# One attention stage on TensorE: three score banks instead of two, the turned maxima and the denominators inside the ring of banks, and the value products of two key tiles back to back

## What is computed

```python
qkv = x @ w_qkv + b_qkv
q, k, v = jnp.split(qkv, 3, axis=-1)          # 16 heads of 32, rope on q and k
attn = jnp.einsum('bhqd,bhkd->bhqk', q, k) * (1.0 / np.sqrt(hd))
attn = jax.nn.softmax(attn, axis=-1)
out = jnp.einsum('bhqk,bhkd->bhqd', attn, v)
```

## Time and profile before

| | |
|---|---|
| median of 3 executions | 3583.11 us (3581.57 to 3583.68) |
| profiled execution, its own time | 3584.84 us |
| profiled execution, span of the core | 3583.0 us |
| mean granted TensorE clock | 0.941 of full speed |
| instructions profiled | 53307 |

### The profile page before, as it was taken

How to read it: one execution, slowest core, us unless ns; L and a number is a source line. 1 busy time by engine, 2 the same in 40 slices (tenths; PEclk the granted TensorE clock), 3 DMA queues, 4 the chain that set the end, 5 groups by cost and what they waited for, 6 DMA issues and landing times. The chain is left out here.

```text
span 3583.0 us, 53307 instructions
## 1 busy us (share of the span) xinstructions
PE 3218.5 (90%) x15180; PEld 2074.7 (58%) x15180; DVE 2025.6 (57%) x3254; ACT 1572.8 (44%) x2848; POOL 1665.3 (46%) x732
## 2 busy tenths in 40 slices
PE   5888789999999999999999994433999998999999
PEld 5666644444444444444444442432888886788887
DVE  2887677878777876878787783533322221322222
ACT  1333217676677766777676773233211111211111
POOL 0222318888788887888788886554100000100000
PEclk9999859999999999999999997766999999999999
DMA  4444449898898988899798987554411211411210
GB/s 168 141 141 142 134 91 194 179 195 189 165 196 183 194 176 171 181 188 199 160 194 178 193 191 166 170 182 161 144 47 47 94 47 49 143 66 47 94 47 24
DMA packets 179320, 508.04 MB, mean 142 GB/s; under 512 B 25914, under 2 KB 43434, under 8 KB 145966
## 3 DMA queue, kind: packets, MB, share of 16 engines
q0 software_dynamic: 36240, 248.53, 34.2%
q1 hardware_dynamic: 132308, 233.59, 21.7%
q10 hardware_dynamic: 10512, 22.81, 1.9%
HBM read 175.18 MB, written 93.62 MB: 75 GB/s over the span
## 5 line engine op out<-in xcount | busy, mean ns | idle before, releaser
L733 DVE TENSOR_REDUCE b_mpart<-b_m 128x1 f32<-128x512 f32 x2136 | 1325.9, 685 | 385.2 <-PE b_m L783 381.3
L672 ACT ACTIVATE b_pt<-b_s 128x512 f32<-128x512 f32 x2048 | 1115.0, 596 | 522.3 <-PE b_s L808 466.4
L711 POOL TENSOR_TENSOR b_acc<-b_acc,b_pt 128x2048 f32<-128x2048 f32 x225 | 1049.2, 4663 | 204.9 <-DMA b_pt<-b_pt 204.2
L808 PE MATMUL b_s<-b_qs,b_ks 98*128 98x512 f32 x2050 | 890.9, 435 | 23.7 <-ACT b_pt L672 23.7
L783 PE MATMUL b_m<-b_ks,b_qs 96*128 96x512 f32 x2136 | 787.2, 415 | 20.5 <-issue 20.2
L808 PEld LDWEIGHTS b_s<-b_qs,b_ks 98*128 98x128 f32 x2050 | 387.3, 189 | 675.3 <-ACT b_pt L672 617.5
L860 PE MATMUL b_o<-b_pt,b_vg 128*32 128x512 f32 x4096 | 549.5, 609 | 0.0
L783 PEld LDWEIGHTS b_m<-b_ks,b_qs 96*128 96x128 f32 x2136 | 417.6, 196 | 96.2 <-DVE b_mpart L733 26.3
L1245 DVE SCALAR_TENSOR_TENSOR d_uf<-d_a,keep_chan,d_sg 128x512 f32<-128x512 f32 x128 | 96.1, 751 | 578.1 <-PE d_a L1273 578.1
L1197 POOL DMA_DIRECT2D d_raw<-in_w_fc x32 | 24.0, 755 | 591.7 <-POOLq L1122 495.7
L1216 ACT ACTIVATE d_sg<-d_g,keep_chan 128x512 f32<-128x512 f32 x128 | 88.1, 689 | 419.7 <-PE d_g L1273 419.7
(11 more groups left out here) (130 smaller groups left out, 3606.6 us busy)
## 6 DMA issues: line engine op xcount, KB each, us to landing
b_pt<-b_pt POOLq DMA_DIRECT2D x225, 1024.0 KB, 8.1
b_ks<-scratch_qk_hi SPq DMA_DIRECT2D x36, 512.0 KB, 5.6
b_qs<-scratch_qk_hi SPq DMA_DIRECT2D x68, 256.0 KB, 5.5
scratch_qk_hi<-a_q_hi SPq DMA_DIRECT2D x64, 256.0 KB, 2.5
scratch_qk_lo<-a_q_lo SPq DMA_DIRECT2D x64, 256.0 KB, 2.8
d_h_hi<-scratch_h_hi SPq DMA_DIRECT2D x16, 1024.0 KB, 7.4
d_h_lo<-scratch_h_lo SPq DMA_DIRECT2D x16, 1024.0 KB, 9.6
d_y<-scratch_y SPq DMA_DIRECT2D x16, 1024.0 KB, 8.0
```

Of the source, the lines that this page charges most:

```text
L672: act.activation(pt[:, kt % RING, h, :], ps_s[:, i % LEAD, :], ACT.Exp, scale=SCALE).then_inc(p_ready, 1)
L711: pool.tensor_tensor(acc[slot][:], acc[slot][:], pt[:, (2 * n + 3) % RING, :, :], ALU.add).then_inc(pool_added, 1)
L733: dve.tensor_reduce(mpart[slot][:, i // 4, i % 4:i % 4 + 1], ps_m[:, i % EARLY, :], AX.X, ALU.max).then_inc(max_done, 1)
L808: pe.matmul(ps_s[:, i % LEAD, :], ks[kslot][0:QR, h, kt * P:(kt + 1) * P], qs[qslot][0:QR, h, :], start=True, stop=True).then_inc(st_done, 1)
```

## The change

Six edits go together.

- `LEAD` goes from 2 to 3: three score banks.
- The bank `ps_d` is gone. The denominators take a place in the round of the three score banks (`SUMS_AT` = 35, between the scores of round 7 and of round 8), and the turned maxima a place in the round of the four maximum banks (`TURN_AT` = 3, behind the third maximum product of the unit two ahead).
- The value products of tiles `kt - 1` and `kt` are issued together at the end of odd rounds; even rounds end without one.
- `ORDER` differs between even and odd rounds: `smsmsmms` and `msmsmsms`.
- ScalarE reads the value products of the unit before (L641) behind the fifth exponential of a unit instead of behind the second, and the denominators ahead of exponential 35 instead of behind exponential 35.
- VectorE splits the turned maximum behind the first three reductions of the unit two ahead, not behind the first eight.

```diff
-LEAD = 2
+LEAD = 3
 EARLY = 4
+TURN_AT = 3
+SUMS_AT = 4 * 8 + LEAD
+
+def score_place(i):
+    return i + (i >= SUMS_AT)
+
+def maximum_bank(n, place):
+    return (65 * (n % 8) + place) % EARLY
...
-        ps_s, ps_m, ps_o, ps_d = m.ps("s", LEAD), m.ps("m", EARLY), m.ps("o", 1), m.ps("d", 1)
+        ps_s, ps_m, ps_o = m.ps("s", LEAD), m.ps("m", EARLY), m.ps("o", 1)
...
-        ORDER, TURN = "smsmmsms", 10
+        ORDER, TURN = ("smsmsmms", "msmsmsms"), 10
...
                     for h in range(GH):
                         i = GH * kt + h
+                        if i == SUMS_AT:
+                            read_denominators(u)
                         act.wait_ge(st_done, STEPS * (u + 1) + i + 1)
-                        if kt == 0 and h == LEAD - 1:
+                        if i == GH:
                             read_products(u)
-                    if kt == D_AT + 1:
-                        read_denominators(u)
...
             def scores(n, kslot, qslot, i):
-                pe.wait_ge(p_ready, STEPS * (n + 1) + i + 1 - LEAD)
+                place = score_place(i)
+                if place == SUMS_AT + LEAD:
+                    pe.wait_ge(d_read, n + 2)
+                else:
+                    last = {0: -2, 1: -1, 2: -3}[i] if i < LEAD else i - LEAD + (SUMS_AT < place < SUMS_AT + LEAD)
+                    pe.wait_ge(p_ready, STEPS * (n + 1) + last + 1)
...
                             at += 1
-                    if kt == TURN:
-                        pe.wait_ge(d_read, u + 2)
-                        turn_max(u + 1)
-                    if kt == 0:
+                            if kt == TURN and at == TURN_AT:
+                                turn_max(u + 1, nj)
+                    if kt % 2 == 0:
+                        continue
+                    if kt == 1:
                         pe.wait_ge(o_read, u + 1)
...
-                    pe.wait_ge(p_ready, STEPS * (u + 1) + GH * (kt + 1))
-                    for h in range(GH):
-                        last = pe.matmul(ps_o[h * HD:(h + 1) * HD, 0, :], vg[kslot][:, kt, h * HD:(h + 1) * HD],
-                                         pt[:, kt % RING, h, :], start=kt == 0, stop=kt == NK - 1)
-                    last.then_inc(pv_done, 1)
+                    for n in (kt - 1, kt):
+                        pe.wait_ge(p_ready, STEPS * (u + 1) + GH * (n + 1))
+                        for h in range(GH):
+                            last = pe.matmul(ps_o[h * HD:(h + 1) * HD, 0, :], vg[kslot][:, n, h * HD:(h + 1) * HD],
+                                             pt[:, n % RING, h, :], start=n == 0, stop=n == NK - 1)
+                        last.then_inc(pv_done, 1)
```

More of the change, by code:

```diff
@@ L508, in stage_b @@
         ITEMS = GH * SUB * 4
-        ORDER, TURN = "smsmmsms", 10
+        ORDER, TURN = ("smsmsmms", "msmsmsms"), 10
         PER = ITEMS // NK
         AHEAD = PER * (NK - TURN)
-        assert ORDER.count("m") == PER and ORDER.count("s") == GH
+        assert all(o.count("m") == PER and o.count("s") == GH for o in ORDER)
         D_AT = 7
+        assert SUMS_AT == GH * (D_AT + 1) + LEAD
         def added(u, n):
@@ L645, in read_denominators @@
                 act.wait_ge(d_out, 16 * (u + 1))
-                act.activation(d_sb[:], ps_d[:, 0, :], ACT.Copy).then_inc(d_read, 1)
+                act.activation(d_sb[:], ps_s[:, SUMS_AT % LEAD, :], ACT.Copy).then_inc(d_read, 1)
             def slot_free(u, kt, pair, j):
@@ L750, in _ @@
             finish_max(0, 0)
-            maxima(1, 1, 0, PER)
-            split_max(0)
-            maxima(1, 1, PER, AHEAD)
+            maxima(1, 1, 0, TURN_AT)
+            split_max(0, 0)
+            maxima(1, 1, TURN_AT, AHEAD)
             def body(u, pair, j):
-                at = AHEAD
-                for kt in range(NK):
-                    if kt == TURN:
-                        finish_max(u + 1, (j + 1) % 2)
-                        at = 0
-                    ahead = 1 if kt < TURN else 2
-                    maxima(u + ahead, (j + ahead) % 2, at, at + PER)
-                    at += PER
-                    if kt == TURN + 1:
-                        split_max(u + 1)
-                    if kt == NK - 2:
-                        invert(u)
+                maxima(u + 1, j + 1, AHEAD, ITEMS)
+                finish_max(u + 1, (j + 1) % 2)
+                maxima(u + 2, j + 2, 0, TURN_AT)
+                split_max(u + 1, j + 1)
+                maxima(u + 2, j + 2, TURN_AT, AHEAD - PER)
+                invert(u)
+                maxima(u + 2, j + 2, AHEAD - PER, AHEAD)
             run(dve, body)
@@ L776, in _, with maxima @@
             pe.sem_inc(st_done, STEPS)
-            def maxima(n, kslot, qslot, lo, hi):
+            def maxima(n, j, kslot, qslot, lo, hi):
                 for i in range(lo, hi):
                     h, s, k = i // 16, i // 4 % 4, i % 4
-                    pe.wait_ge(max_done, ITEMS * (n + 1) + i + 1 - EARLY)
-                    pe.matmul(ps_m[:, i % EARLY, :], qs[qslot][0:KR, h, s * P:(s + 1) * P],
+                    place = i + (i >= TURN_AT)
+                    if place == TURN_AT + EARLY:
+                        pe.wait_ge(mlo_ready, n + 1)
+                    else:
+                        last = i - EARLY + (TURN_AT < place < TURN_AT + EARLY)
+                        pe.wait_ge(max_done, ITEMS * (n + 1) + last + 1)
+                    pe.matmul(ps_m[:, maximum_bank(j, place), :], qs[qslot][0:KR, h, s * P:(s + 1) * P],
                               ks[kslot][0:KR, h, k * TB:(k + 1) * TB], start=True, stop=True).then_inc(max_ps, 1)
@@ L788, in denominators @@
                 pe.wait_ge(pool_added, added(u - 1, PAIRS - 1))
-                pe.wait_ge(mlo_ready, u + 2)
-                pe.wait_ge(d_read, u + 1)
                 for h in range(GH):
-                    last = pe.matmul(ps_d[h * HD:(h + 1) * HD, 0, :], ones[:, 0:HD], acc[slot][:, h, :], start=True, stop=True)
+                    last = pe.matmul(ps_s[h * HD:(h + 1) * HD, SUMS_AT % LEAD, :], ones[:, 0:HD], acc[slot][:, h, :], start=True, stop=True)
                 last.then_inc(d_ps, 1)
@@ L814, in _ @@
             operands(0, 0)
-            maxima(0, 0, 0, 0, ITEMS)
+            maxima(0, 0, 0, 0, 0, ITEMS)
             operands(1, 0)
-            maxima(1, 0, 1, 0, PER)
-            turn_max(0)
-            maxima(1, 0, 1, PER, AHEAD)
+            maxima(1, 1, 0, 1, 0, TURN_AT)
+            turn_max(0, 0)
+            maxima(1, 1, 0, 1, TURN_AT, AHEAD)
             pe.wait_ge(ones_ready, 3)
@@ L835, in body @@
                         at = 0
-                    for what in ORDER:
+                    for what in ORDER[kt % 2]:
                         if what == "s":
```

27 lines of the change are left out of this document (15 added, 12 removed).

## The result

Seven executions of the changed kernel had a median of 3566.20 us (3560.90 to 3573.88), seven of the kernel before on the same chip 3583.11 (3579.60 to 3584.86): a ratio of 0.9959, interval 0.9946 to 0.9972. The gain is 17 us, 0.4%, where I had forecast 35 (3548 us). It lies in the range (3504 to 3582), but at rival (b), not at the forecast. The profiled execution took 3560.9 us, 23.9 less than the profiled one of before, with a span of 3559.1. It is the fastest of its seven, as the profiled one of before is nearly the slowest of its own, so the profiles differ by more than the medians. One of the six executions of the queries later took 14096.67 us, and without it that median would be 3559.62 us.

A forecast was written before the change was run, and what follows sets the result against it. TensorE sets the pace, GpSimd with its DMAs close behind. TensorE's unit falls 1.95 us to 48.8, waits eat 0.9, leaving 1.05; over 32 units about 35 us gained, giving 3548 us (range 3504 to 3582).

The forecast's parts named there:

- rival (b): GpSimd and DMA already at their limit over four units; gain 0 to 0.8 us a unit, 3558 to 3583; chance 0.21.
- The pair of rounds: TensorE: pairing value products makes two rounds take 5.86 us instead of 6.20, saving 0.34 a pair, 2.7 a unit.
- 0.15, 0.45 and 0.43: TensorE's unit: microseconds for scores delayed by the denominators' read, the moved read of value products, and the maxima's turn.
- alone it gains nothing: Third score bank: lets ScalarE work through the pair, but no gain by itself since TensorE already starts without a hole.
- The place and the kind of the wait: Exponentials wait for GpSimd's add or a fold, 25 to 35 us in all; maximum products don't wait each pair.
- I give the four units 1.0, 1.9, 0.7 and 0: 0.9 on the mean: TensorE's loss to GpSimd's lateness over four units, three with key/value loads; leaves 1.05 of 1.95 us gained a unit.
- one stretch of GpSimd's chain: Sixth fold's release to the unit's last add: GpSimd and DMA need 25.5 us, TensorE's way shrinks from 26.0 to 24.3.
- ScalarE comes 1.2 us late, and of that TensorE feels about 1.0: At the slot freed by a unit's last add: ScalarE's wait for GpSimd passed on to TensorE, whose bank had 0.45 spare.
- Rival (a): TensorE alone decides, the ring of eight tiles evening out the rest; 1.95 to 2.7 us a unit, 3497 to 3521; chance 0.22.
- Rival (c): Slower: fold landings grow; about 12.3 us in three heavy units uses up the gain, 13.1 gives 3602; chance 0.07.

The follow-up runs named there:

- queries later: Changed kernel with two key/value pieces loaded per unit, queries' load moved behind tile 1's value products and pieces behind tiles 5 and 7: 3559.98 us, ratio 0.9938.
- unpaired kernel: Changed kernel with value products back behind every round, old order and early read of value products; third bank and new places stay: 3577.92 us, ratio 0.9988.
- unpaired kernels: Changed kernel with value products back behind every round, with key/value loads whole (3577.92 us) or cut to four columns (3554.54 us).
- no pieces: Changed kernel with in-loop loads of the next group's keys and values cut to four columns, so later outputs are wrong: 3501.59 us, ratio 0.9778.
- last add first: Changed kernel with GpSimd adding a unit's last pair before issuing the next unit's first fold: 3656.52 us, ratio 1.0202.
- even pieces: Changed kernel with eight key/value pieces spread two to a unit instead of three, three, two and none, first sooner, second later: 3542.15 us, ratio 0.9881.
- half adds: Changed kernel with GpSimd adding only two of four heads, the other denominators left at ones, loads and folds whole: 3509.45 us, ratio 0.9797.

## Why the prediction was right in sign and short in size

**The pair of rounds: right, in part by luck.** 5.82 us for 5.86, 1.85 for both groups and the way back for 1.88. The unhindered unit took 48.30 for 48.8: the pairs give 8 x 0.04 = 0.3 more than forecast, and what I had put at 0.15, 0.45 and 0.43 is 0.86 together, for 1.03. In TensorE's timeline of such units the denominators cost nothing beyond their 0.88, the read of the value products 0.33, and the pair of rounds with the turn takes 6.32, 0.50 more than a plain one (in the unpaired kernel the moved turn costs 0.12, as before). But "alone it gains nothing", of the third bank, was wrong: with the new places it brought a round from 3.10 to 3.05. The unpaired kernels part the gain in another way than I did. From 50.67 to 50.04 us, 0.63 a unit, TensorE's own work fell by bank and places, which my sum had at a loss of 0.48 (0.15 and the turn's 0.33); from 50.04 to 48.22, 1.8 a unit, by the pairs and the read moved with them, which my sum had at 2.44 (2.72 less 0.28). Two errors stood against each other.

**The place and the kind of the wait: right.** ScalarE stands before the slot that the unit's last add frees, for GpSimd, and no maximum product waits in each pair.

**The failed step: "I give the four units 1.0, 1.9, 0.7 and 0: 0.9 on the mean".** It says that of a gain of 1.95 us a unit 0.9 is eaten; inside the passes 2.5 us a unit were eaten out of 2.5 gained, and ScalarE's waits came to 65 us where I said 25 to 35. The path and the wait were the right ones; the term for what they cost was too small. Two things were wrong in it.

First, I followed one stretch of GpSimd's chain, from the sixth fold to the last add, and compared that with TensorE's. The whole unit has to be compared as well. Two folds are under way at most, since fold n + 2 stands behind add n in GpSimd's program. A unit's chain is then: from the first fold to the second over the last add of the unit before, 0.6 + 4.6; three times a landing, 0.2 and an add of 4.57 (second, fourth and sixth fold; the others lie beside them); and the first pair, 4.6. That is 24.1 us and three landings, an estimate from these rows. They took 8.57 us on the mean of these folds in the changed kernel: 49.8 us. With no pieces they sum to 22.7 instead of 25.7: 46.8, under TensorE's 48.3, and the waits inside the passes went. With the last add first they sum to 29.7: 53.8, and the units took 53.96. Units with three pieces had 27.4 to 28.3 in the three landings, about 52; those with two had 24.7, those without 22.4. So three units of four need more than TensorE's new 48.3, and two of them more than its old 50.75 as well, which the lighter units repaid before. At 48.3 nothing is left to repay with: GpSimd's folds, which left 1.2 us behind the value products on the mean before (4.0 at most), leave 2.1 behind, up to 8.2. The landings of the kernel before, 25.2 us in the three folds, would have shown this (49.3 for the chain); the busy share of 81 to 84% that I read hides it, because a wait for a landing counts as idle.

The sum is not the whole of it. Inside the passes the changed kernel's units took 50.80 us, 1.0 more than the 49.8. With the even pieces the sum is 48.0, and no unit of the four has more than 48.4, yet units took 50.23 in the execution profiled, and ScalarE waited at tiles 6 and 7 for a last fold that landed in 11.1 us: the stretch that I had followed can hold ScalarE by one late landing, though the whole unit would fit. How much of the 2.5 us is the one and how much the other no run tells apart.

Secondly, "ScalarE comes 1.2 us late, and of that TensorE feels about 1.0" prices the hole alone. Twelve times the granted clock fell behind one inside the stage, 1.7 us or more each: of the 55 us that the stage lost, 19 are the clock's.

Rival (b), "GpSimd and DMA already run at their own limit over four units", is what happened, in the sense of a serial chain; it had 0.21. A limit of the DMA engines' bandwidth was not: with half adds they moved more. Rival (a) was TensorE's due: with the chain relieved the kernel reached 3502 and 3509, in (a)'s 3497 to 3521. Rival (c), a landing grown to 12.3 us in the heavy units, didn't come: the mean landing went from 8.49 to 8.73. The last add first shows that such a landing is real elsewhere.

What stays open: why a second fold 0.6 us behind the first lands in 12 us (two of 1 MB under way together, or the way they are queued; not the pieces, since in units without any it took 11.4 to 12.9), and how far the clock alone would go, since no run took a hole away and left the wait. The executions of the changed kernel lie 13 us apart, those of before 5; holes and clock falls that come in one execution and not in another would do that, but only one execution of each was profiled.

## What to carry to other kernels

Before the engine that sets the pace is made faster, work out the serial chain of the engine that follows it over a whole period (landing plus the operation that needs it, times the links that can't overlap), for the heaviest and the lightest part of the period, and compare that with the new pace; a busy share of 82% can be a chain with nothing to spare. Where the sum fits, look at the single latest landing too. Price a new wait of TensorE with what the granted clock shows behind such holes, here 1.7 us on top of holes of 1.6 to 3.6, behind nearly every one of them. And when a chain is rearranged, look at which transfers then leave together: two edits that let GpSimd reach its second fold sooner bunched its folds and gave half, or more than all, of the gain back, while spreading the loads over the units cost nothing.

## What the runs showed of the hardware

- Behind a hole of 2.83 us on TensorE the granted clock was 1.2 GHz from within 788 to 790 us to within 792 to 794, with TensorE busy all the while; the first 1.7 us behind the hole still ran at 2.4 GHz. Of twelve falls inside the stage ten cost 1.7 us and two 2.9 and 3.4. A hole of 2.5 us (at 2020) brought none, one of 1.6 us (behind 838) did.
- Two accumulating DMAs of 1 MB within SBUF, issued 0.6 us apart: the second landed in 12.1 us on the mean (11.4 to 12.9 in the units without loads of keys and values, where the first took 7.0), where it took 9.4 when 5.5 us lay between. With 2.1 us between on the mean it still took 12.3.
- The stage moved 193 GB/s with half adds, at the same landing of 8.5 us as at 186: between these two the landing didn't grow with the rate. Without the pieces, at 173 GB/s, it was 7.6.
- A third score bank and the new places took a round of the same matmuls from 3.10 to 3.05 us, though TensorE had no idle time in the record before.
